# Decoder attention: the attended rows turned, divided and joined on VectorE in 32x32 blocks

## The chip, the cores and the metric

The kernel runs on one core of a Trainium2 chip. The metric is the device time of one execution in microseconds (us). The engines are TensorE (PE, with its weight loads as PEld), VectorE (DVE), ScalarE (ACT), GpSimd (POOL) and SyncE (SP), which issues the transfers. Each runs its own instructions in the order in which the program gives them, and they meet at semaphores.

## The reference

A decoder of four layers, then a cross attention and a mixture of experts, each with a residual and a norm. The change is in the decoder's attention alone:

```python
L, D, H, F = (4, 256, 16, 1024); HD = D // H
def mha(x, mask, Wi, bi, Wo, bo):
    B, T, _ = x.shape
    q, k, v = jnp.split(x @ Wi.T + bi, 3, axis=-1)
    # each: reshape(B, T, H, HD).transpose(0, 2, 1, 3)
    scores = jnp.einsum('bhqd,bhkd->bhqk', q, k) / math.sqrt(HD)
    attn = jax.nn.softmax(scores + mask[None], axis=-1)
    out = jnp.einsum('bhqk,bhkd->bhqd', attn, v)
    return out.transpose(0, 2, 1, 3).reshape(B, T, D) @ Wo.T + bo
for i in range(L):
    x = x + mha(layer_norm(x, ln1_w[i], ln1_b[i]), mask, ...)
    h = gelu(layer_norm(x, ln2_w[i], ln2_b[i]) @ ffn1_w[i].T + ffn1_b[i])
    x = x + (h @ ffn2_w[i].T + ffn2_b[i])
```

x is 16 x 256 tokens of 256 features, in float32.

## The kernel before

The 4096 tokens go in eight groups of 512 (`GT`), four layers long: 32 items n. The order of work is written out by hand for each engine in a function `body`, and one body works at four items: it prepares item n + 1 (`ahead`: first norm, queries and keys, maxima of the first two clusters), attends for item n (`front`), brings item n - 1 from its attended rows to the hidden layer (`back`), and shrinks the hidden layer of item n - 2 (`tail`). A steady body has all four. Three bodies in each layer also bring in the next layer's weights: `swap` 1 those of queries, keys and values, 2 those of the output projection, 3 those of the hidden layer; ACT and DVE make two float16 parts of each.

The 16 heads go in four clusters c of four heads (`C`), and the scores of a cluster in three stages s (`ST`). PE's `row_scores(n, c, s)` writes scores into the one bank pair `maxima_pair`; DVE's `maxima(n, c, s)` reduces them to the maximum of each row, and only then may PE write the next. PE's `key_scores(n, c, s)` writes the scores the other way round, maximum included, into the one pair `scores_pair`; ACT's `exps` makes the probabilities, and only then may PE write the next. POOL clears what lies ahead in time (`past_only`). PE's `attend(n, c)` multiplies with the values into the bank `O`: head u of the cluster has the partitions 32u to 32u + 31, of which 16 hold its attended features and the next one the sum of its probabilities, since `VS` has ones beside the values. So `O` is (head, feature) x 512 tokens. ACT's `out_rows(n, c)` copies it into `OTs[:, c, :]`.

In the next body the four copies are turned twice on PE. `turn_outputs` (line 735) makes four transposes of 128x128 into one bank for each 128 tokens t: tokens on the partitions. DVE's `outputs` (line 1160) takes the reciprocal of the sums and multiplies into `On`. `turn(..., "OT", k, ...)` (line 644) turns `On` back, half k of the 256 features at a time, into a bank; ACT's `outputs_high` and DVE's `outputs_low` add the values' bias and leave two float16 parts in `oT`, and PE's `attended` is the output projection.

All that PE writes for one reader, but scores and `O`, goes round a ring of three banks. `tiles_of` lists the uses in a body's order, and `free_tile` lets PE wait for the readers of the use three places before. After `attended` come DVE's addition into x, the second norm (`norm2_stats`, `norm2_root`, `norm2_scaled`), its turn on PE, the hidden layer (`hidden`, eight banks) with ACT's `gelu`, and the low parts by POOL (four) and DVE (four, `hidden_low`, line 1135, at the end of DVE's body). `norm1` for item n + 2 stands just ahead of these.

Of the kernel before, what the change touches and what calls it, by code (L numbers as in the profile page):

```python
# [17 lines left out]
P = 128  # L18
D = 256
# [331 lines left out]
def decoder(nc, sb, sem, psum, shared, dram):  # L351
# [36 lines left out]
    mx, mrow, PR, OTs, On, oT = (shared[k] for k in ("mx", "mrow", "PR", "OTs", "On", "oT"))  # L388
    rden = shared["rden"]
# [3 lines left out]
    def sig(name, per, unit=1):  # L393
        return Signal(sem("d_" + name), per, unit)
# [19 lines left out]
    OS_ps, rd_in, on_in = sig("OS_ps", TT), sig("rd_in", TT), sig("on_in", TT)  # L414
    OT_ps, oh, ol = sig("OT_ps", KD), sig("oh", KD), sig("ol", KD)
# [17 lines left out]
        "OS": [(on_in, 1)], "OT": [(oh, 1), (ol, 1)], "OP": [(xo, 1)], "T2": [(xf2, 1), (xh2, 1)],  # L433
# [3 lines left out]
    ROUND = {"T1": 1, "QK": 1, "MT0": 1, "MT1": 1, "V": 0, "MT2": 0, "MT3": 0, "OS": -1, "OT": -1, "OP": -1,  # L437
# [197 lines left out]
    def _(pe):  # L635
        for s in (T1_ps, V_ps, QK_ps, M_ps, MT_ps, S_ps, O_ps, OS_ps, OT_ps, OP_ps, T2_ps, H_ps, Y_ps):
            pe.sem_inc(s.sem, s.credit())
# [97 lines left out]
        def turn_outputs(kind, n, t):  # L735

            bank = free_tile(pe, kind, n, "OS", t)
            if t == 0:
                pe.wait_ge(o_in.sem, o_in.after(n - 1))
            for c in range(C):  # L740
                last = pe.transpose(bank[:, c * P:(c + 1) * P], OTs[:, c, t * P:(t + 1) * P], ident[:, :])
            last.then_inc(OS_ps.sem, 1)

# [27 lines left out]
        def body(kind, n, g, swap, l, ahead, front, back, tail):  # L771
# [9 lines left out]
            if back:  # L781
                turn_outputs(kind, n, 0)
                turn_outputs(kind, n, 1)
            if front:
                key_scores(n, 0, 1)
            if back:
                turn_outputs(kind, n, 2)
                turn_outputs(kind, n, 3)
            if front:
                row_scores(n, 2, 1)  # L790
                values(kind, n, 1)
            if back:
                pe.wait_ge(on_in.sem, on_in.after(n - 1))
                turn(kind, n, "OT", 0, OT_ps, On)
# [6 lines left out]
            if back:  # L801
                turn(kind, n, "OT", 1, OT_ps, On)
# [91 lines left out]
    def _(act):  # L894
# [58 lines left out]
        def outputs_high(kind, n, k):  # L953
            act.wait_ge(OT_ps.sem, OT_ps.after(n - 1, k + 1))
            if k == 0:
                act.wait_ge(OP_ps.sem, OP_ps.after(n - 2))
            act.activation(oT[0][:, k, :], tile(kind, "OT", k)[:, :], ACT.Identity, bias=value_col(n - 1, k))\  # L957
               .then_inc(oh.sem, 1)
# [163 lines left out]
    def _(dve):  # L1122
        for s in (w_lo, qb_ready, ln1_steps, z1, xl1, mx_in, rd_in, on_in, ol, xo, ln2_steps, z2, xl2, y_x, h_l[1],
                  *start.stats_in, start.rooted, start.zf, start.z1):
            dve.sem_inc(s.sem, s.credit())
# [34 lines left out]
        def outputs(kind, n, t):  # L1160
            dve.wait_ge(OS_ps.sem, OS_ps.after(n - 1, t + 1))
            bank = tile(kind, "OS", t)[:, :].rearrange("p (h d) -> p h d", h=H)
            if t == 0:
                dve.wait_ge(OT_ps.sem, OT_ps.after(n - 2))
            dve.reciprocal(rden[:, t, :], bank[:, :, HD]).then_inc(rd_in.sem, 1)
            dve.wait_ge(rd_in.sem, rd_in.after(n - 1, t + 1))
            dve.tensor_tensor(On[:, t, :].rearrange("p (h d) -> p h d", h=H), bank[:, :, 0:HD],
                              rden[:, t, :].unsqueeze(2).to_broadcast([P, H, HD]), ALU.mult)\
               .then_inc(on_in.sem, 1)

# [15 lines left out]
        def outputs_low(kind, n, k):  # L1186
            dve.wait_ge(oh.sem, oh.after(n - 1, k + 1))
            if k == 0:
                dve.wait_ge(OP_ps.sem, OP_ps.after(n - 2))
            dve.scalar_tensor_tensor(oT[1][:, k, :], tile(kind, "OT", k)[:, :], value_col(n - 1, k), oT[0][:, k, :],  # L1190
                                     ALU.add, ALU.subtract).then_inc(ol.sem, 1)
# [24 lines left out]
        def body(kind, n, g, swap, l, ahead, front, back, tail):  # L1216
# [14 lines left out]
            if back:  # L1231
                outputs(kind, n, 0)
                outputs(kind, n, 1)
                outputs(kind, n, 2)
                outputs(kind, n, 3)
# [29 lines left out]
            if back:  # L1265
                norm2_root(n, group(g, -1))
                norm2_scaled(n, group(g, -1))
            if swap == 2:
                weights(l, "o")
# [16 lines left out]
            if tail:  # L1286
                shrunk(kind, n, group(g, -2), 3)
            if swap == 3:
                weights(l, "f2")
            if ahead:  # L1290
                maxima(n + 1, 1, 0)
                maxima(n + 1, 1, 1)
                maxima(n + 1, 1, 2)
                if not (kind is STEADY and isinstance(n, int) and n + 2 >= L * NG):
                    if kind is PRE:
                        dve.wait_ge(s_x, 16)
                    norm1(n + 2, group(g, 2))
            if kind is LAST:
# [1634 lines left out]
def laid_out(inputs):  # L2933
# [7 lines left out]

    def columns(b):
        return b.reshape(-1, P).T
# [8 lines left out]
        stationary(f["attn_out_proj_w"][l].T),  # L2952
# [5 lines left out]
    value_cols = np.concatenate([*(columns(b[2 * D:]) for b in f["attn_in_proj_b"]), columns(f["xattn_bv"])], 1)  # L2958
# [35 lines left out]
```

## Time and profile before

| | |
|---|---|
| time, median of three runs | 3473.02 us (3469.25 to 3474.62) |
| the profiled execution: time, span | 3473.01 us, 3471.3 us |
| mean granted clock of TensorE | 0.970 |
| busy in the span: PE, DVE, ACT, POOL | 94%, 77%, 66%, 47% |
| ends of the last `out_rows`, first and last item | 89.8 us, 1768.4 us |
| between these, 23 of 31 bodies | 52.4 to 52.7 us each |
| three with `swap` 1 | 55.74, 57.73, 58.51 us |
| four with `swap` 3 | 63.35, 63.12, 63.62, 63.63 us |
| the last | 46.16 us |

The decoder takes the first half of the span. The lengths of its bodies are read from the starts of ACT's fourth `out_rows` in each. A busy PE is read with care: the ends of matmuls are modelled, so that a short wait can be hidden by the record of the matmul ahead of it, and the starts of the next instructions tell more. Idle time of an engine that nothing waits for costs nothing.

### The profile page before, as it was taken

What the parts mean: (1) busy time and instruction counts of PE and PEld (TensorE: products, weight loads), DVE (VectorE), ACT (ScalarE), POOL (GpSimd) and SP (SyncE); (2) the same over time, 40 slices, a digit from 0 to 9 for tenths busy, and PEclk for the clock granted to TensorE, in tenths of its full rate; (3) what the DMA queues carried; (4) which work ended last, traced back from release to release, by engine and by line L of the source; (5) the groups of instructions that cost most, each with busy time, mean ns of one, the idle gap of its engine ahead of it and who ended that gap; (6) DMA issues with size and microseconds to landing.
All of it is one profiled execution on the core that took longest, in us unless ns stands there. A gap on an engine that the chain in (4) does not pass through costs nothing. (4 is left out here: it accounts for less than half of the span.)

```text
span 3471.3 us, 76257 instructions
## 1 busy us (share of the span) xinstructions
PE 3252.6 (94%) x29568; PEld 2158.1 (62%) x29568; DVE 2675.1 (77%) x5237; ACT 2299.8 (66%) x3540; POOL 1648.4 (47%) x1612
## 2 busy tenths in 40 slices
PE   5899999999999999999986887899999999999998
PEld 2566665666656666566653554566666666666665
DVE  4777777777777777777677888898888888888877
ACT  3677776777777777777745665566666666666665
POOL 2354453544535445353444433564444444544475
PEclk8999999999999999999997999899999999999999
DMA  3110111101111011110011212100000000000001
GB/s 117 37 38 29 41 52 34 38 29 41 49 37 38 29 41 49 37 38 29 29 45 59 65 55 69 59 13 27 27 1 27 1 27 1 27 1 27 1 13 37
DMA packets 104485, 122.87 MB, mean 35 GB/s; under 512 B 20320, under 2 KB 92256, under 8 KB 101984
## 3 DMA queue, kind: packets, MB, share of 16 engines
q1 hardware_dynamic: 104128, 118.00, 10.4%
q8 instruction: 237, 3.88, 0.5%
q14 instruction: 120, 0.98, 0.1%
HBM read 49.35 MB, written 8.39 MB: 17 GB/s over the span
## 5 line engine op out<-in xcount | busy, mean ns | idle before, releaser
L2830 POOL TENSOR_TENSOR e_hT<-e_h,e_hT 128x512 f16<-128x512 f32 x512 | 613.5, 1200 | 605.7 <-ACT e_hT L2579 581.9
L1335 POOL TENSOR_SCALAR_AFFINE_SELECT PR<-PR 128x512 f32<-128x512 f32 (+1 forms) x384 | 307.4, 805 | 833.9 <-ACT PR L1002 832.1
L2573 ACT ACTIVATE e_h<-e_h,e_b 128x512 f32<-128x512 f32 x512 | 365.4, 714 | 416.3 <-DVE e_h L2659 416.3
L1214 DVE TENSOR_REDUCE mx<-maxima_pair 128x4 f16<-128x1024 f32 (+1 forms) x384 | 469.2, 1222 | 213.5 <-PE maxima_pair L694 213.4
L93 PE MATMUL bank<-xT,w_half 128*128 128x512 f16 x2400 | 568.5, 387 | 5.7 <-DVE xT L1157 4.2
L1002 ACT ACTIVATE PR<-scores_pair 128x1024 f32<-128x1024 f32 x384 | 391.6, 1020 | 102.4 <-PE scores_pair L706 101.9
L93 PEld LDWEIGHTS bank<-xT,w_half 128*128 128x128 f16 x2400 | 227.6, 99 | 272.6 <-issue 31.3
L2517 PE MATMUL bank<-VS,e_hT 128*128 128x256 f16 x3072 | 389.1, 273 | 6.2 <-DVE VS L2622 4.6
L2517 PE MATMUL bank<-e_w,e_hT 128*128 128x256 f16 x3072 | 388.7, 273 | 4.3 <-POOL e_hT L2830 4.1
L93 PE MATMUL bank<-w_half,hT 128*128 128x256 f16 x3072 | 364.3, 276 | 8.0 <-ACT oT L957 5.8
L2517 PEld LDWEIGHTS bank<-VS,e_hT 128*128 128x128 f16 x3072 | 300.2, 98 | 113.1 <-DVE VS L2622 5.1
L2517 PEld LDWEIGHTS bank<-e_w,e_hT 128*128 128x128 f16 x3072 | 300.7, 98 | 109.6 <-POOL e_hT L2830 6.3
L93 PEld LDWEIGHTS bank<-w_half,hT 128*128 128x128 f16 x3072 | 298.0, 99 | 63.4 <-issue 6.7
L2579 ACT ACTIVATE e_hT<-e_h 128x512 f16<-128x512 f32 x512 | 322.5, 630 | 16.2
L2669 DVE SCALAR_TENSOR_TENSOR x<-e_b,expert_weight,x 128x256 f32<-128x256 f32 x224 | 239.2, 1117 | 0.0
L1355 POOL TENSOR_TENSOR x<-x,spare 128x256 f32<-128x256 f32 x256 | 205.2, 837 | 18.9 <-DVE z L160 18.9
L1344 POOL TENSOR_TENSOR QK<-qk,QK 128x512 f16<-128x512 f32 x128 | 149.1, 1165 | 114.4 <-ACT qk L930 105.1
L995 ACT ACTIVATE spare<-bank,cols 128x512 f32<-128x512 f32 x256 | 172.7, 683 | 38.9 <-PE bank L93 38.4
L690 PE MATMUL maxima_pair<-KS,QS 63*128 63x256 f16 (+1 forms) x2048 | 152.3, 248 | 47.4 <-DVE mx L1214 41.7
L2659 DVE TENSOR_TENSOR e_h<-maxima_pair,e_common 128x512 f32<-128x512 f32 x192 | 131.1, 688 | 78.4 <-PE maxima_pair L2495 35.1
L2659 DVE TENSOR_TENSOR e_h<-scores_pair,e_common 128x512 f32<-128x512 f32 x192 | 131.9, 687 | 66.4 <-PE scores_pair L2495 50.3
L986 ACT ACTIVATE hT<-bank,cols 128x512 f16<-128x512 f32 x256 | 171.8, 686 | 8.0 <-PE bank L93 4.3
(215 smaller groups left out, 6352.2 us busy)
## 6 DMA issues: line engine op xcount, KB each, us to landing
QS<-QK SPq DMA_DIRECT2D x240, 128.0 KB, 2.1
KS<-QK SPq DMA_DIRECT2D x192, 128.0 KB, 2.1
PR<-in_expert_weights SPq DMA_DIRECT2D x16, 1024.0 KB, 5.1
stage<-in_weights SPq DMA_DIRECT2D x48, 256.0 KB, 3.4
xT<-in_x SPq DMA_DIRECT2D x8, 512.0 KB, 3.8
xT_f<-xT SPq DMA_DIRECT2D x8, 512.0 KB, 3.7
stage<-xT_f SPq DMA_DIRECT2D x4, 1024.0 KB, 5.2
out<-stage SPq DMA_DIRECT2D x8, 512.0 KB, 3.7
```

Source lines behind the costliest of these rows:

```text
L93: last = pe.matmul(out, stat(a, k), mov(b, k), start=(k == 0 and n == 0), stop=(k == tiles - 1 and n == 2))
L995: act.activation(h32[:, m % NH32, :], tile(kind, "H", m)[:, :], ACT.Gelu, bias=cols[:, COL["f1b"] + m:COL["f1b"] + m + 1], scale=1.0 / WS) ...
L1002: act.activation(PR[c % 2][:, s, :], SC[:, :], ACT.Exp).then_inc(p_in.sem, 1)
L1214: dve.tensor_reduce(out, src, AX.X, ALU.max, negate=True).then_inc(mx_in.sem, 1)
L1335: pool.affine_select(blocks, blocks, [[0, x], [1, P]], base=0, channel_multiplier=-1, compare_op=ALU.is_ge, fill=nothing).then_inc(past.se ...
L1355: last = pool.tensor_tensor(x[:, bass.ds(g * TT + t, 1), :], x[:, bass.ds(g * TT + t, 1), :], rows[:, row, :].unsqueeze(1), ALU.add)
L2517: last = pe.matmul(y_bank(tile), hT[r % 2][a][:, f, tile * P:(tile + 1) * P], w2[e % 2][b][:, i + f * NI, :], start=i == f == n == 0 and u ...
L2573: act.activation(h32[r % 2][:, j, :], h32[r % 2][:, j, :], ACT.Gelu, bias=b1[:, e, m:m + 1], scale=1.0 / WS)\
L2579: act.activation(hT[r % 2][0][:, f, t * GT:(t + 1) * GT], h32[r % 2][:, j, :], ACT.Copy).then_inc(h_h.sem, 1)
L2659: dve.tensor_tensor(out, bank_of(r, p), part, ALU.add).then_inc(added.sem, 1)
L2669: dve.scalar_tensor_tensor(x[:, n:n + 1, :], b2[e % 2][:, :, :], weight[:, at:at + 1], x[:, n:n + 1, :], ALU.mult, ALU.add).then_inc(bias_ ...
L2830: pool.tensor_tensor(hT[r % 2][1][:, f, part], h32[r % 2][:, j, :], hT[r % 2][0][:, f, part], ALU.subtract)\
```

## The change

The turns of the attended rows on PE are gone, and with them two uses of the ring of banks (`OS`, `OT`). ACT's copy in `OTs[:, c, :]` stays as it is. DVE's new `divide(n, c)` transposes each 32x32 block of it into `turned`: now a block has 32 tokens on its partitions and one head's 32 rows in its columns. The reciprocal of column 16 and a multiplication with the 16 features go into half of the 32 columns of each block in `divided`, which is a view of `On`; a cluster c takes the half c % 2. `join_outputs(n, k)` transposes two divided clusters in blocks once more, into `OTs[:, 2k, :]`: features on the partitions. ACT and DVE read that in place of a bank. The features come out in another order, so the output projection's weights and the values' bias are put in that order on the host.

The clusters are worked at as they come: `divide(n, 0)` after the second norm, `divide(n, 1)` and the first join ahead of the maxima of the next item's second cluster, `divide(n, 2)` after `norm1`, `divide(n, 3)` and the second join at the opening of the next body. ACT's `out_rows` waits until the rows that it overwrites have been read.

```diff
-        "OS": [(on_in, 1)], "OT": [(oh, 1), (ol, 1)], "OP": [(xo, 1)], "T2": [(xf2, 1), (xh2, 1)],
+        "OP": [(xo, 1)], "T2": [(xf2, 1), (xh2, 1)],
...
-        out = f(("V", 0)) + b(("OS", 0, 1, 2, 3)) + f(("V", 1)) + b(("OT", 0)) + a(("T1", 0)) + b(("OT", 1))
+        out = f(("V", 0, 1)) + a(("T1", 0))
...
         def out_rows(n, c):
             act.wait_ge(O_ps.sem, O_ps.after(n, c + 1))
-            if c == 0:
-                act.wait_ge(OS_ps.sem, OS_ps.after(n - 1))
+            if c % 2 == 0:
+                act.wait_ge(oh.sem, oh.after(n - 1, c // 2 + 1))
+                act.wait_ge(ol.sem, ol.after(n - 1, c // 2 + 1))
+            else:
+                act.wait_ge(turned_in.sem, turned_in.after(n - 1, c + 1))
             act.activation(OTs[:, c, :], O[:, :], ACT.Copy).then_inc(o_in.sem, 1)
...
+        def divide(n, c):
+            dve.wait_ge(o_in.sem, o_in.after(n, c + 1))
+            dve.wait_ge(on_in.sem, on_in.after(n, c))
+            dve.transpose(turned[:, :], OTs[:, c, :]).then_inc(turned_in.sem, 1)
+            blocks = turned[:, :].rearrange("p (b r) -> p b r", r=SQ)
+            dve.wait_ge(turned_in.sem, turned_in.after(n, c + 1))
+            dve.reciprocal(rden[:, c, :], blocks[:, :, HD]).then_inc(rd_in.sem, 1)
+            dve.wait_ge(rd_in.sem, rd_in.after(n, c + 1))
+            dve.wait_ge(joined.sem, joined.after(n - 1, c // 2 + 1))
+            to = divided[:, c // 2, :].rearrange("p (b r) -> p b r", r=SQ)[:, :, c % 2 * HD:(c % 2 + 1) * HD]
+            dve.tensor_tensor(to, blocks[:, :, 0:HD], rden[:, c, :].unsqueeze(2).to_broadcast([P, BL, HD]), ALU.mult)\
                .then_inc(on_in.sem, 1)
+        def join_outputs(n, k):
+            dve.wait_ge(on_in.sem, on_in.after(n, 2 * k + 2))
+            dve.transpose(OTs[:, 2 * k, :], divided[:, k, :]).then_inc(joined.sem, 1)
```

On PE at the opening of a steady body the turns stood between the values and the second `key_scores` and `row_scores`. Before, `scores_pair` is `key_scores`, `maxima_pair` is `row_scores`, and `OTs` is a turn:

```order
L93 MATMUL bank<-w_half,xT_1 128x256
L741 MATMUL bank<-ident,OTs 128x128 x8
L706 MATMUL scores_pair<-QS,KS 128x256 x4
L741 MATMUL bank<-ident,OTs 128x128 x8
L690 MATMUL maxima_pair<-KS,QS 128x256 x4
L694 MATMUL maxima_pair<-ident_b,mask_q 128x2x64 x4
```

and now:

```order
L93 MATMUL bank<-w_half,xT_0 128x256 x2
L93 MATMUL bank<-w_half,xT_1 128x256
L711 MATMUL scores_pair<-QS,KS 128x256 x4
L695 MATMUL maxima_pair<-KS,QS 128x256 x4
L699 MATMUL maxima_pair<-ident_b,mask_q 128x2x64 x4
```

The second `key_scores` and `row_scores` follow the values at once.

On DVE, across the end of a steady body and the opening of the next (`z` is the end of the first norm, `hT` is `hidden_low`, `mx` a maximum), before; the last two rows stand three times more ahead of the next maximum:

```order
L160 TENSOR_SCALAR z<-x,norm_mean_var,norm_root 128x256 x4
L1140 TENSOR_TENSOR hT<-spare,hT 128x512 x4
L1214 TENSOR_REDUCE mx<-maxima_pair 128x4
L1165 RECIPROCAL rden<-bank 128x16
L1167 TENSOR_TENSOR On<-bank,rden 128x256
```

and now:

```order
L160 TENSOR_SCALAR z<-x,norm_mean_var,norm_root 128x256 x4
L1150 STREAM_TRANSPOSE turned<-OTs 128x512
L1153 RECIPROCAL rden<-turned 128x16
L1157 TENSOR_TENSOR On<-turned,rden 128x16x16
L1126 TENSOR_TENSOR hT<-spare,hT 128x512 x4
L1208 TENSOR_REDUCE mx<-maxima_pair 128x4
L1150 STREAM_TRANSPOSE turned<-OTs 128x512
L1153 RECIPROCAL rden<-turned 128x16
L1157 TENSOR_TENSOR On<-turned,rden 128x16x16
L1163 STREAM_TRANSPOSE OTs<-On 128x512
L1208 TENSOR_REDUCE mx<-maxima_pair 128x4
```

One cluster is divided ahead of `hidden_low`, and another one divided and joined between the first two maxima.

On DVE after the second norm of a steady body (`x` is the addition of `shrunk`), before:

```order
L160 TENSOR_SCALAR z<-x,norm_mean_var,norm_root 128x256 x4
L1183 SCALAR_TENSOR_TENSOR x<-bank,x 128x256 x2
L1214 TENSOR_REDUCE mx<-maxima_pair 128x4
L1157 TENSOR_TENSOR xT_1<-xT_1,xT_0 128x512
L1214 TENSOR_REDUCE mx<-maxima_pair 128x4
```

and now:

```order
L160 TENSOR_SCALAR z<-x,norm_mean_var,norm_root 128x256 x4
L1150 STREAM_TRANSPOSE turned<-OTs 128x512
L1153 RECIPROCAL rden<-turned 128x16
L1157 TENSOR_TENSOR On<-turned,rden 128x16x16
L1177 SCALAR_TENSOR_TENSOR x<-bank,x 128x256 x2
L1208 TENSOR_REDUCE mx<-maxima_pair 128x4
```

A division stands ahead of the two additions, which free banks of the ring.

## Rows read from the trace of the kernel before

**Rows 1.** Busy time of bodies: length, PE, PEld, DVE, ACT, POOL, clock, DMA

```profile
691.47:743.92 52.45, 52.21 (x570) 34.39 (x566) 38.30 (x86) 39.56 (x59) 24.77 (x28) 1.00 0.10 32
415.19:470.93 55.74, 52.36 (x570) 34.43 (x566) 40.36 (x90) 41.22 (x62) 24.78 (x28) 1.00 0.19 63
849.39:907.12 57.73, 54.03 (x568) 35.30 (x566) 40.70 (x89) 41.23 (x62) 24.89 (x28) 0.97 0.19 61
523.46:586.58 63.12, 54.93 (x569) 34.97 (x566) 45.66 (x94) 43.76 (x67) 25.92 (x28) 0.95 0.14 46
```

**Rows 2.** Groups over the decoder: busy us, mean ns | idle before

```profile
L741 PE MATMUL bank<-ident,OTs 128*128 128x128 f32 x512 | 75.2, 281 | 11.8 <-DVE On L1167 7.5 <-ACT OTs L1008 0.8
L649 PE MATMUL bank<-ident,On 128*128 128x128 f32 x256 | 41.4, 287 | 0.8 <-DVE On L1167 0.8
L1167 DVE TENSOR_TENSOR On<-bank,rden 128x256 f32<-128x256 f32 x128 | 54.3, 424 | 4.4
L1165 DVE RECIPROCAL rden<-bank 128x16 f32<-128x16 f32 x128 | 31.6, 247 | 1.0 <-PE bank L741 1.0
L1157 DVE TENSOR_TENSOR xT<-xT 128x512 f16<-128x512 f32 x64 | 44.5, 696 | 59.0 <-ACT xT L913 59.0
```

**Rows 3.** Timeline of TensorE, a steady body's opening: start, length

```profile
691.47 0.39 PE L706 MATMUL scores_pair<-QS,KS 64*128 64x256 f16 x4
...
693.45 1.04 PE L741 MATMUL bank<-ident,OTs 128*128 128x128 f32 x8
694.61 0.39 PE L706 MATMUL scores_pair<-QS,KS 64*128 64x256 f16 x4
...
696.36 0.39 PE L690 MATMUL maxima_pair<-KS,QS 63*128 63x256 f16 x4
...
699.32 0.39 PE L690 MATMUL maxima_pair<-KS,QS 63*128 63x128 f16 x8
...
700.38 2.78 PE L93 MATMUL bank<-w_half,hT 128*128 128x256 f16 x24
```

**Rows 4.** Timeline of ScalarE, the same opening

```profile
692.24 1.28 ACT L1002 ACT_TABLE_LOAD   x1
693.53 1.02 ACT L1002 ACTIVATE PR<-scores_pair 128x1024 f32<-128x1024 f32 x1
```

**Rows 5.** Timeline of VectorE, the same opening

```profile
691.47 2.49 DVE L1140 TENSOR_TENSOR hT<-spare,hT 128x512 f16<-128x512 f32 x4
693.88 1.22 DVE L1214 TENSOR_REDUCE mx<-maxima_pair 128x4 f16<-128x1024 f32 x1
```

**Rows 6.** Timeline of all engines, the turn of the second norm

```profile
720.21 0.42 DVE L1183 SCALAR_TENSOR_TENSOR x<-bank,x 128x256 f32<-128x256 f32 x1
...
721.32 0.60 PE L649 MATMUL bank<-ident,z 128*128 128x128 f32 x4
```

**Rows 7.** Timeline of all engines, ahead of the next cluster's maxima

```profile
729.79 0.41 DVE L1183 SCALAR_TENSOR_TENSOR x<-bank,x 128x256 f32<-128x256 f32 x1
...
730.75 1.23 DVE L1214 TENSOR_REDUCE mx<-maxima_pair 128x4 f16<-128x1024 f32 x1 [0.55 <-PE maxima_pair L694]
...
733.34 0.39 PE L690 MATMUL maxima_pair<-KS,QS 63*128 63x256 f16 x4
```

**Rows 8.** Timeline of all engines, a collision of POOL and DVE

```profile
715.78 1.09 POOL L1335 TENSOR_SCALAR_AFFINE_SELECT PR<-PR 128x1024 f32<-128x1024 f32 x1 [1.35 <-ACT PR L1002]
...
715.88 1.00 DVE L150 SCALAR_TENSOR_TENSOR norm_root<-norm_slope,norm_root 128x4 f32<-128x4 f32 x1
```

**Rows 9.** Busy time around a fall of the clock, columns as in rows 1

```profile
421.55:425.00 3.45, 1.72 (x21) 1.33 (x19) 1.75 (x3) 2.90 (x6) 0.00 (x0) 1.00 0.00 0
858.45:861.87 3.42, 1.30 (x19) 1.06 (x20) 3.36 (x5) 2.25 (x5) 1.09 (x1) 1.00 0.00 0
861.87:865.29 3.42, 3.42 (x19) 2.44 (x17) 1.94 (x3) 1.30 (x2) 0.00 (x0) 0.50 0.00 0
```

**Rows 10.** Timeline of TensorE, opening of a body with a layer's first weights

```profile
860.57 0.40 PE L690 MATMUL maxima_pair<-KS,QS 63*128 63x128 f16 x8 [3.07 <-DVE mx L1214]
```

More of the change, by code:

```diff
@@ L387, in decoder @@
     qk32 = shared["qk32"]
-    mx, mrow, PR, OTs, On, oT = (shared[k] for k in ("mx", "mrow", "PR", "OTs", "On", "oT"))
-    rden = shared["rden"]
+    mx, mrow, PR, OTs, oT = (shared[k] for k in ("mx", "mrow", "PR", "OTs", "oT"))
+    SQ = 32
+    BL = GT // SQ
+    turned = sb("turned", [P, GT], F32)
+    rden = shared["rden"].rearrange("p c k -> p (c k)").rearrange("p (c k) -> p c k", c=C)
+    divided = shared["On"].rearrange("p t d -> p (t d)").rearrange("p (k n) -> p k n", k=KD)
+    assert C == 2 * KD and BL == H
     h32 = shared["spare"][:, 0:NH32 * GT].rearrange("p (m n) -> p m n", m=NH32)
@@ L635, in _ @@
     def _(pe):
-        for s in (T1_ps, V_ps, QK_ps, M_ps, MT_ps, S_ps, O_ps, OS_ps, OT_ps, OP_ps, T2_ps, H_ps, Y_ps):
+        for s in (T1_ps, V_ps, QK_ps, M_ps, MT_ps, S_ps, O_ps, OP_ps, T2_ps, H_ps, Y_ps):
             pe.sem_inc(s.sem, s.credit())
@@ L733, in attend @@
             last.then_inc(O_ps.sem, 1)
[L735 to L742, printed above, removed]
         def attended(kind, n, k):
@@ L800, in body @@
                 row_scores(n, 2, 2)
-            if back:
-                turn(kind, n, "OT", 1, OT_ps, On)
             if tail:
@@ L953, in outputs_high @@
         def outputs_high(kind, n, k):
-            act.wait_ge(OT_ps.sem, OT_ps.after(n - 1, k + 1))
+            act.wait_ge(joined.sem, joined.after(n - 1, k + 1))
             if k == 0:
                 act.wait_ge(OP_ps.sem, OP_ps.after(n - 2))
-            act.activation(oT[0][:, k, :], tile(kind, "OT", k)[:, :], ACT.Identity, bias=value_col(n - 1, k))\
+            act.activation(oT[0][:, k, :], OTs[:, 2 * k, :], ACT.Identity, bias=value_col(n - 1, k))\
                .then_inc(oh.sem, 1)
@@ L1122, in _ @@
     def _(dve):
-        for s in (w_lo, qb_ready, ln1_steps, z1, xl1, mx_in, rd_in, on_in, ol, xo, ln2_steps, z2, xl2, y_x, h_l[1],
+        for s in (w_lo, qb_ready, ln1_steps, z1, xl1, mx_in, turned_in, rd_in, on_in, joined, ol, xo, ln2_steps, z2, xl2, y_x, h_l[1],
                   *start.stats_in, start.rooted, start.zf, start.z1):
@@ L1231, in body @@
             if back:
[L1232 to L1235, printed above, removed]
+                divide(n - 1, 3)
+                join_outputs(n - 1, 1)
             if swap == 1:
@@ L1267, in body @@
                 norm2_scaled(n, group(g, -1))
+            if front:
+                divide(n, 0)
             if swap == 2:
@@ L1287, in body @@
                 shrunk(kind, n, group(g, -2), 3)
+            if front:
+                divide(n, 1)
+                join_outputs(n, 0)
             if swap == 3:
@@ L1297, in body @@
                     norm1(n + 2, group(g, 2))
+            if front:
+                divide(n, 2)
             if kind is LAST:
@@ L2940, in stationary @@
         return w.reshape(-1, P, w.shape[1]).transpose(1, 0, 2).reshape(P, -1)
+    turned = np.arange(D).reshape(KD, 2, C, HD).transpose(0, 2, 1, 3).reshape(D)
     def columns(b):
@@ L2957, in laid_out @@
     rows = np.stack([f["attn_out_proj_b"], f["attn_ffn2_b"]], 1)
-    value_cols = np.concatenate([*(columns(b[2 * D:]) for b in f["attn_in_proj_b"]), columns(f["xattn_bv"])], 1)
+    value_cols = np.concatenate([*(columns(b[2 * D:][turned]) for b in f["attn_in_proj_b"]), columns(f["xattn_bv"])], 1)
     wide = [(0, D - E_CTX), (0, 0)]
```

30 lines of the change are left out of this document (5 added, 25 removed).

## The prediction

> **What bounds the kernel now.** I read the busy times of single decoder bodies first, then the timelines of TensorE (PE), ScalarE (ACT) and VectorE (DVE) through one body, and at the end the clock. In a steady body PE shows 52.21 of 52.45 us busy at clock 1.00, DVE 38.30, ACT 39.56, POOL 24.77 [rows 1]. So PE sets the length of these bodies; 23 of the 31 listed in the table of the section on the profile have it. DVE's idle quarter is not spread evenly, though. I call S the start of a body on PE, 691.47 in [rows 3], and count from it. At S + 0.00 DVE is still at four `hidden_low` operations of the body before, which take 2.49 us; only then does it start the maximum of cluster 2, stage 0, at S + 2.41, for 1.22 us [rows 5]. PE reaches the next `row_scores`, which needs that maximum, at S + 4.89 (696.36). ACT, after a table load of 1.28 us, ends the first exponential at S + 3.08 [rows 4], and the second `key_scores` starts at S + 3.14 (694.61) [rows 3]. So at the opening ACT and DVE are late already, and the turns of the outputs on PE fill the time in which it would wait for them. Everywhere else I ask the same of each place that gets new work on DVE: how much later may DVE be there until PE notices?
>
> **What is removed.** Per body 16 transposes of the attended rows and 8 of the divided ones: 75.2 and 41.4 us in all [rows 2], 116.6 us or 3.64 us in each of the 32 bodies. On DVE four reciprocals of 0.247 us and four divisions of 0.424 us go from the opening [rows 2], and four of each come back elsewhere. ACT keeps its number of operations; the two biased copies of the attended features now read SBUF instead of a bank.
>
> **What is added.** Per body six block transposes of 128x512 on DVE. None stands in the trace. The nearest rows by shape are the DVE subtractions of 128x512, 0.696 us [rows 2]. Half of the columns take 0.424 us (128x256, [rows 2]); 1024 columns take 1.22 us [rows 5]. So T, the time of one, lies between 0.42 (two columns in the time of one) and 1.22 (two passes); I take 0.70, the row of the same shape. The Trainium skill, "Vector Engine (DVE) Microarchitecture Reference", section 3.8 on the reshape front-end, says that the transpose is pipelined to one element per cycle and lane; no run here shows it, and by it the upper end would fall away and the sum stay.
>
> A `divide` is then T, a reciprocal (0.25), a division (0.42), each waiting for the last: in [rows 5] an operation that waits for nothing starts 0.08 before the record of the one ahead ends (691.47 + 2.49 against 693.88), and I give 0.03 for a hand-over inside. This makes 0.70 + 0.03 + 0.25 + 0.04 + 0.42 - 0.08 = 1.36 us. `join_outputs` adds 0.73: 2.09 for both. Three places decide.
>
> *The opening.* `divide(n, 2)` now stands ahead of the four `hidden_low`: they end 1.36 later, the maximum starts at S + 3.77 and ends at 4.99, and PE's `row_scores` starts at S + 5.05. PE itself has done its first scores and values by S + 1.98 (693.45 [rows 3]), waits for ACT until 3.14, does 0.31 us of `key_scores`, and waits for DVE until 5.05: it loses 1.16 + 1.60 us. Behind that maximum DVE does `divide` of cluster 3 and the second join (2.09) where four reciprocals and divisions stood, so the next maximum starts at 3.77 + 1.14 + 2.09 = 7.00 and ends at 8.22: the third `row_scores` at S + 8.28, against 7.85 (699.32) before. It needs 0.54 us; the second turn of divided rows that followed it (0.52) is gone, and `shrunk` starts at S + 8.82, against 8.91 (700.38) before. So of 3.64 us removed, 0.09 us is left.
>
> *After the second norm.* `divide(n, 0)` stands ahead of the addition of `shrunk` 1 (720.21 to 720.63), which frees the bank for the turn of the second norm. That turn starts at 721.32 [rows 6], so the addition had 0.69 us to spare; 1.36 less 0.64 (with a hand-over of 0.05) makes 0.72 us of wait.
>
> *Ahead of the next cluster's maxima.* `divide(n, 1)` and the first join follow the addition that ends at 730.20; the maximum of cluster 1, stage 0, starts at 730.12 + 2.09 = 732.21, against 730.75, and with its 1.23 us is over at 733.44; PE wants it at 733.34 [rows 7]. That is 0.1 us, and I take 0.2, since the division there may meet POOL. In [rows 8] a DVE operation of two SBUF operands and 4 columns took 1.00 us: until POOL's operation ended. The division used to read a bank and now reads two SBUF operands. The Trainium skill, "SBUF — State Buffer", section "Who interferes with whom", has this as a lock between such an instruction and a GpSimd one that reads SBUF, and says that an instruction with one SBUF input takes no part in it; the row bears out the first half, and by the rule the six transposes are exempt.
>
> Sum of a steady body: -0.09 + 0.72 + 0.20 = +0.83 us; for 23 bodies +19.1. In the three bodies with the first weights of a layer (415.19, 849.39) the third `row_scores` already waits 3.07 us [rows 10] for maxima behind the weights on DVE, which wait for ACT and for the values; that stays, 0.16 later, and the turn's 0.52 is saved: -0.35 + 0.72 + 0.20, three times, +1.7. In the four with the hidden layer's weights (523.46) DVE waits for ACT's weights in the third place, which covers the join; I put +0.9 for each, +3.6.
>
> **The clock.** PE was at full clock (1.00) through the steady bodies. In 858.45 to 861.87 PE was busy 1.30 of 3.42 us, and the granted clock stood at 0.50, the lower level of 1.2 GHz, for the next 3.42 us; after 421.55 to 425.00, with 1.72 of 3.45 busy, it did not fall [rows 9]. The new opening has some 0.4 us busy in the 3.07 us from S + 1.98. It looks more like the first. Two bodies of the same work, one with such a fall and one without, last 57.73 and 55.74 us [rows 1]: a fall costs 1.99 us. Here some 0.6 of it falls into the wait for the third `row_scores`. Of the three bodies with that wait two show a fall; I take half of the steady bodies at 1.5 us: 23 x 0.75 = +17.
>
> All together 19.1 + 1.7 + 3.6 + 17 = +41.4 us. The profiled execution took 3473.01 us (span 3471.3), the median of the runs is 3473.02, so nothing is to be scaled: 3514.4.
>
> **Rivals.**
> 1. *The clock holds.* Same waits, no fall in the openings: 3473.0 + 24.4 = 3497.4. For it: each of the two waits is shorter than the 3.07 us of [rows 10], and work lies between them. Against: the sum of both in one stretch.
> 2. *The block transpose is slow.* At T = 1.22 the opening holds three of them in a chain (+1.56), the second place one (+0.52), the third two (+1.04): +3.12 per body beyond the 0.83, 23 x 3.95 = 91, falls in nearly all openings (+28) and some 16 in the other bodies: about 3608. For it: a 32-bit element may take two passes. Against: every DVE row follows its columns.
> 3. *The block transpose is quick, and the kernel gets faster.* At T = 0.42 the opening ends 0.84 earlier (-0.93), the second place costs 0.44, the third nothing: -0.49 per body, no long wait, 23 x -0.49 = -11: 3462. The point: without falls of the clock a body breaks even where 4 x (0.70 - T) = 0.63, T = 0.54. Against: no DVE row of 512 columns is that quick.
> 4. *The removed turns show in full*, DVE having room all along as its 73% busy suggests: 3473.0 - 116.6 = 3356. Against: the order of DVE's queue, worked out above. Partial forms lie between.
>
> **How the numbers follow.** Forecast with falls of the clock 0.43; clock holds 0.22; slow transpose 0.12; quick 0.13; full or large gain 0.04; the small terms cancel and nothing can be seen 0.06. A measurement of this kernel tells about 0.2% (7 us) from no change. Faster: quick and full, 0.17, less 0.01 of "quick" that ends within 0.2%: 0.16. Same: 0.06 and that 0.01, 0.07. Slower: 0.77. The range must hold 0.8: the forecast, the holding clock, no change (0.71), most of the quick case and the lower part of the slow one, so 3460 to 3600.
>
> **What would show it.** STREAM_TRANSPOSE of 128x512 at 0.70 us, 192 of them in the decoder. In a steady body the second `row_scores` 5.0 us and the third 8.3 us after the body's start, each released by DVE's maximum; the turn of the second norm released by DVE's addition, 0.7 us late; POOL's and ACT's lists unchanged; bodies of 53.3 us at full clock and about 55 where the clock falls behind the opening. DVE busy goes up by 32 x (6 x 0.70) = 134 us, PE's down by less than 117. Wrong would be: a transpose under 0.54 us, a steady body under 52.4, or PE without waits at the opening.

## The result: 84.7 us slower, twice the forecast loss

The changed kernel takes 3557.57 us (median of four runs, 3556.77 to 3560.1) against 3472.9 us: 1.0249 times the kernel before, 95% interval 1.0237 to 1.0261. The forecast was 3514.4. The direction held, the size did not: +84.7 us where the sum said +41.4.

The profiled execution (span 3556.0 us, of before 3471.3) has the whole difference in the decoder. The last `out_rows` of the decoder starts at 1850.6 us instead of 1768.4 (the table ahead of the prediction calls these starts ends), +82.2 us; what follows takes 1705.4 us instead of 1702.9. Busy time of the engines on the page of the changed kernel:

```profile
PE 3209.3 (90%) x28800; PEld 2097.2 (59%) x28800; DVE 2819.8 (79%) x5429; ACT 2304.8 (65%) x3540; POOL 1675.4 (47%) x1612
```

PE has 43 us less to do and DVE 145 us more, still with a fifth of the span free. The groups that are new, over the decoder (busy us, mean ns | idle before):

```profile
L1150 DVE STREAM_TRANSPOSE turned<-OTs 128x512 f32<-128x512 f32 x128 | 89.9, 702 | 0.0
L1163 DVE STREAM_TRANSPOSE OTs<-On 128x512 f32<-128x512 f32 x64 | 45.5, 711 | 2.2
L1157 DVE TENSOR_TENSOR On<-turned,rden 128x256 f32<-128x256 f32 x128 | 68.8, 538 | 4.9 <-DVE rden L1153 0.5
L1153 DVE RECIPROCAL rden<-turned 128x16 f32<-128x16 f32 x128 | 32.5, 254 | 4.4
```

The block transpose, the price that no row of before had, takes 0.70 us as taken. The division rose from 0.424 [rows 2] to 0.538 us in the mean, which comes back below.

Busy time of bodies, columns as in [rows 1]: a steady body in which the clock held, the next one, in which it fell, one with a layer's first weights (`swap` 1), one with the hidden layer's (`swap` 3):

```profile
723.45:777.35 53.90, 49.59 (x545) 31.75 (x542) 42.89 (x92) 39.74 (x59) 25.59 (x28) 1.00 0.09 31
777.35:832.68 55.33, 51.15 (x544) 32.53 (x541) 42.87 (x91) 39.73 (x59) 25.59 (x28) 0.97 0.09 30
429.46:490.82 61.36, 54.19 (x544) 34.15 (x541) 45.32 (x96) 41.28 (x62) 25.87 (x28) 0.89 0.18 57
546.68:613.07 66.39, 53.49 (x544) 32.91 (x540) 50.45 (x99) 43.81 (x67) 27.40 (x28) 0.92 0.13 43
```

Against 52.45, 55.74 and 63.12 [rows 1] every kind of body is longer, though each has 24 transposes less on PE. In the steady body PE is busy for 49.59 of 53.90 us; the other 4.31 us are five waits. The three of the opening, on TensorE, answer to [rows 3] (S is 723.45):

```profile
726.59 0.39 PE L711 MATMUL scores_pair<-QS,KS 64*128 64x256 f16 x4 [1.00 <-ACT PR L985]
728.50 0.39 PE L695 MATMUL maxima_pair<-KS,QS 63*128 63x256 f16 x4 [1.52 <-DVE mx L1208]
...
731.72 0.40 PE L695 MATMUL maxima_pair<-KS,QS 63*128 63x128 f16 x8 [0.53 <-DVE mx L1208]
731.96 0.38 PE L699 MATMUL maxima_pair<-ident_b,mask_q 64*128 64x256 bf16 x4
732.27 2.79 PE L93 MATMUL bank<-w_half,hT 128*128 128x256 f16 x24
```

The second `row_scores` comes at S + 5.05, the third at S + 8.27, `shrunk` at S + 8.82: the forecast said 5.05, 8.28 and 8.82. The other two waits, the turn of the second norm [rows 6] and the place ahead of the next cluster's maxima [rows 7], all engines:

```profile
754.05 0.63 PE L654 MATMUL bank<-ident,z 128*128 128x128 f32 x4 [0.66 <-DVE x L1177]
...
763.91 0.94 DVE L1157 TENSOR_TENSOR On<-turned,rden 128x256 f32<-128x256 f32 x1
763.94 0.63 POOL L1334 TENSOR_SCALAR_AFFINE_SELECT PR<-PR 128x512 f32<-128x512 f32 x1
...
766.77 0.39 PE L695 MATMUL maxima_pair<-KS,QS 63*128 63x256 f16 x4 [0.60 <-DVE mx L1208]
```

The division next to POOL's selection took 0.94 us, and PE waits 0.60 us for the maximum behind it. In the next body the opening has the same first two waits, and then the clock falls. Busy time before and after that moment, columns as above:

```profile
778.97:782.38 3.41, 0.91 (x9) 0.33 (x7) 3.41 (x6) 2.97 (x4) 1.56 (x2) 1.00 0.00 0
782.38:785.79 3.41, 3.39 (x21) 2.39 (x22) 3.08 (x5) 0.00 (x0) 0.28 (x1) 0.50 0.03 7
```

PE was busy for 0.91 of 3.41 us at clock 1.00; then it has its work back to back, at 0.50, the lower level of 1.2 GHz. This happens in 17 of the 23 steady bodies. Summed over the decoder from 150 us on, the clock stands at 0.50 for 136.5 us, before the change for 37.5 us.

### The profile page after: what moved, and what is told of

It reads as the page before. It is cut to its first block and busy times, and to the rows that moved or that the text cites. A ratio compares the mean times of both kernels' runs of the same rounds, so it can differ in the third digit from the quotient of the medians.

```text
span 3556.0 us, 75196 instructions
## 1 busy us (share of the span) xinstructions
PE 3209.3 (90%) x28800; PEld 2097.2 (59%) x28800; DVE 2819.8 (79%) x5429; ACT 2304.8 (65%) x3540; POOL 1675.4 (47%) x1612
## 5 line engine op out<-in xcount | busy, mean ns | idle before, releaser
L1334 POOL TENSOR_SCALAR_AFFINE_SELECT PR<-PR 128x512 f32<-128x512 f32 (+1 forms) x384 | 325.1, 850 | 881.6 <-ACT PR L985 877.3
L711 PE MATMUL scores_pair<-QS,KS 64*128 64x256 f16 (+1 forms) x2048 | 152.5, 248 | 37.6 <-ACT PR L985 37.0
```

The lines of the kernel that those rows point to most:

```text
L1334: pool.affine_select(blocks, blocks, [[0, x], [1, P]], base=0, channel_multiplier=-1, compare_op=ALU.is_ge, fill=nothing).then_inc(past.se ...
```

## The experiments

The theory after the result: nothing is lost because DVE has more to do, but because each piece stands ahead of something that PE needs soon (place); a part of the loss is the clock, which falls where the pieces hold PE up. The rival: DVE's 3.6 us more per body are paid wherever they stand (load). All times are medians over three rounds, and ratios are to the kernel before in the same job.

| kernel | us | ratio, 95% interval | steady body, clock up | steady bodies with a fall |
|---|---|---|---|---|
| before | 3470 to 3473 | 1 | 52.45 | 0 of 23 |
| changed | 3557.57 | 1.0249 (1.0237 to 1.0261) | 53.90 | 17 |
| `div0` | 3510.22 | 1.0116 (1.0101 to 1.0131) | 52.60 | 15 |
| `div1` | 3534.62 | 1.0184 (1.0169 to 1.0199) | 53.23 | 18 |
| `div2` | 3482.42 | 1.0033 (1.0023 to 1.0043) | 52.52 | 0 |
| `late1` | 3549.33 | 1.0226 (1.0211 to 1.0242) | 53.77 | 17 |
| `quiet` | 3539.34 | 1.0195 (1.0178 to 1.0212) | 53.49 | 18 |
| `busy` | 3527.81 | 1.0164 (1.0149 to 1.0179) | 53.90 | 0 |
| `busyo` | 3543.80 | 1.0206 (1.0189 to 1.0223) | 53.89 | 14 |
| `free` | 3432.87 | 0.9892 (0.9877 to 0.9907) | 50.89 | 0 |
| `all3` | 3451.59 | 0.9942 (0.9927 to 0.9957) | 51.59 | 0 |
| `all3late` | 3438.35 | 0.9906 (0.9889 to 0.9922) | 51.10 | 0 |
| `best` | 3421.52 | 0.9858 (0.9843 to 0.9873) | 50.52 | 0 |

### One piece at a time, behind a maximum

In `div2` only the division that stood ahead of `hidden_low` moves:

```diff
                 maxima(n + 1, 1, 1)
+            if front:
+                divide(n, 2)
+            if ahead:
                 maxima(n + 1, 1, 2)
...
-            if front:
-                divide(n, 2)
             if kind is LAST:
```

> divide(n, 2) stands between the maxima of stages 1 and 2 of the next item's cluster 1, where DVE waited 2.0 us for PE, not ahead of hidden_low; nothing else differs from the changed kernel. Theory 'place': the opening's chain on DVE is 1.36 us shorter, second row_scores at 3.7 and third at 6.9 us after the body's start (5.05 and 8.27 before this edit), steady body 52.5 us, and as the waits of the opening shrink to 1.2, 0.2 and 0.6 us the clock does not fall behind it: 23 x (54.98 - 52.5) = 57 us less, some 7 more in the bodies with weights, 3493 us. Rival 'load': DVE simply has too much to do, the wait turns up again at the next maxima, 3550 or more.

Measured 3482.42 us, 75 us less than the changed kernel. TensorE at the opening of a steady body, S = 698.01:

```profile
701.15 0.39 PE L711 MATMUL scores_pair<-QS,KS 64*128 64x256 f16 x4 [1.00 <-ACT PR L985]
701.69 0.39 PE L695 MATMUL maxima_pair<-KS,QS 63*128 63x256 f16 x4 [0.15 <-DVE mx L1208]
...
704.91 0.40 PE L695 MATMUL maxima_pair<-KS,QS 63*128 63x128 f16 x8 [0.53 <-DVE mx L1208]
```

The wait for DVE of 1.52 us is 0.15 us, and with it every fall of the clock is gone from the steady bodies. One division (1.36 us in the forecast), at the end of a body, was worth 1.38 us in each body and the falls besides. The kernel is 11 us faster than the 3493 expected, mainly because the seven bodies with weights got 18 us shorter where some 7 were written.

In `div0` and `div1` the pieces after the second norm and ahead of the next cluster's maxima move in the same way:

```diff
-            if front:
-                divide(n, 0)
...
                 maxima(n + 1, 0, 0)
+            if front:
+                divide(n, 0)
```

> divide(n, 0) stands behind the first maximum of the next item, not ahead of the two additions that free banks. Theory 'place': the wait of 0.75 us for the turn of the second norm is gone in all steady bodies, 53.15 us where the clock does not fall; falls behind the opening stay. 23 x 0.75 and some 5 in the others: 3535 us. Rival 'load': the 1.36 us delay the next low part or maximum and PE waits there, 3555 us.

```diff
-            if front:
-                divide(n, 1)
-                join_outputs(n, 0)
...
                 maxima(n + 1, 1, 0)
+            if front:
+                divide(n, 1)
+                join_outputs(n, 0)
+            if ahead:
                 maxima(n + 1, 1, 1)
```

> divide(n, 1) and the first join stand behind the maximum of stage 0 of the next item's cluster 1, not ahead of it. Theory 'place': the wait of 0.60 to 0.70 us at the following row_scores is gone, 53.2 us where the clock does not fall, 3538 us in all. Rival 'load': the maximum of stage 1 or 2 comes late in its place, 3555 us.

`div1` came out as expected: the body is 0.67 us shorter, what the third place cost, and the falls stay. The division there still takes 0.87 us in the median, but no step of PE waits for it now. `div0` did better than expected, 3510 where 3535 was written: the wait at the turn is gone, as it should be, but the wait in the third place also went from 0.60 to 0.16 us, though nothing was changed there. All engines around it in a body of `div0`:

```profile
694.72 0.50 DVE L1157 TENSOR_TENSOR On<-turned,rden 128x256 f32<-128x256 f32 x1
694.88 0.83 POOL L1334 TENSOR_SCALAR_AFFINE_SELECT PR<-PR 128x512 f32<-128x512 f32 x1
...
697.13 0.39 PE L695 MATMUL maxima_pair<-KS,QS 63*128 63x256 f16 x4 [0.16 <-DVE mx L1208]
```

DVE comes 0.16 us ahead of POOL, and it is POOL's selection that is stretched, from 0.63 to 0.83 us. So the place's price seems to hang on who comes first there; the next run asks whether POOL makes it. The 0.44 us, in 23 bodies, are 10 of the 25 us; the falls in the steady bodies cost 17.5 us in place of 24.1, and what else came was not followed up.

### POOL out of the division's way

```diff
-                past_only(n, 3, 0)
+                past_only(n, 3, 0, 16)
+                past_only(n, 3, 1, 16)
             if ahead:
                 query_key_low(n + 1, 3)
             if front:
-                past_only(n, 3, 1)
                 past_only(n, 3, 2)
```

> The changed kernel with VectorE's and TensorE's program as it is, and GpSimd made quiet where divide(n, 1) falls: the causal selection of the first two parts of chunk 3 covers 16 of the 128 columns (the rest of the selection is left out), and query_key_low of tile 3 stands behind these two. Theory (collision: the division of divide(n, 1), 0.94 us where it starts beside GpSimd's writes, is what made the third place cost 0.70 us, not 0.20): the division takes 0.42 to 0.52 us, the row_scores behind it waits 0.10 to 0.20 us in place of 0.59, and a steady body without a fall of the clock is 53.3 to 53.5 us in place of 53.9; the whole is 3530 to 3552 us if falls come as often. Rival (the place itself, that the piece has four instructions ahead of the maximum whatever GpSimd does): wait 0.5 to 0.6 us, body 53.8 to 53.9 us.

The wait and the body came out as the collision theory has it; the division, 0.54 us, is just over the 0.52 expected, since it still begins beside a selection. All engines:

```profile
871.68 0.54 DVE L1157 TENSOR_TENSOR On<-turned,rden 128x256 f32<-128x256 f32 x1
871.70 0.63 POOL L1334 TENSOR_SCALAR_AFFINE_SELECT PR<-PR 128x64 f32<-128x64 f32 x2
...
874.13 0.39 PE L695 MATMUL maxima_pair<-KS,QS 63*128 63x256 f16 x4 [0.20 <-DVE mx L1208]
```

The wait is 0.20 instead of 0.60 us and the body 53.49 instead of 53.90 us. The Trainium skill, "SBUF — State Buffer", section "Who interferes with whom", calls this an exclusive lock between a VectorE instruction with two SBUF inputs and a GpSimd one that reads SBUF, in which the order of issue decides who is held up. The row of `div0` agrees, where POOL's selection is the one held up. In the changed kernel DVE's record begins 0.03 us ahead of POOL's and DVE is held up, so at that distance the records don't tell who was first. The joins, block transposes with one input, stay between 0.695 and 0.715 us, as the rule has it.

### The opening's own piece

In `late1` `divide(n - 1, 3)` and the second join go behind the second maximum of the opening:

```diff
-            if back:
-                divide(n - 1, 3)
-                join_outputs(n - 1, 1)
...
                 maxima(n, 2, 1)
+            if back:
+                divide(n - 1, 3)
+                join_outputs(n - 1, 1)
```

> The changed kernel with divide(n - 1, 3) and join_outputs(n - 1, 1) behind maxima(n, 2, 1) in the opening, all else as it is: the opening's piece alone. Theory (place): the second row_scores of chunk 2 still comes at 5.05 us after the body's first key_scores, since divide(n, 2) at the end of the body before makes it late; the third comes at 6.9 to 7.1 us in place of 8.27, but the output projection then waits for VectorE's outputs_low and starts at some 12.6 us, 0.3 to 0.5 us sooner than in the changed kernel. A steady body without a fall 53.4 to 53.7 us; falls in fewer of the bodies; 3515 to 3550 us. Rival (the opening's piece is the one that costs most, as it stands ahead of the maxima on which TensorE's first scores rest): second row_scores at 3.9 us or sooner, body 52.5 to 52.8 us, 3480 to 3505 us.

TensorE in a body with S = 782.24:

```profile
787.29 0.39 PE L695 MATMUL maxima_pair<-KS,QS 63*128 63x256 f16 x4 [1.52 <-DVE mx L1208]
...
794.80 0.93 PE L93 MATMUL bank<-w_half,oT 128*128 128x256 f16 x7 [0.41 <-issue]
```

The second `row_scores` is where it was, at S + 5.05, so the rival falls. The third comes at S + 7.58, where 6.9 to 7.1 was expected. The output projection starts at S + 12.56, as expected, but that is only 0.13 us sooner than in the changed kernel (S + 12.70), not 0.3 to 0.5: a miss in my reading of where it stood. Its wait takes the place of the one removed. The body is 53.77 us, just over the 53.7 expected, and falls came as often as before, in 17 bodies; that expectation was wrong too. With the division ahead of `hidden_low` still there, the waits of 1.00 and 1.52 us stay, and the falls with them.

### What the clock takes

`busy` leaves all waits as they are and gives PE matmuls that nobody reads, in the two waits of the opening:

```diff
                 values(kind, n, 0)
+                idle_matmuls(kind, n, 4)
                 key_scores(n, 0, 1)
+                idle_matmuls(kind, n, 6)
                 row_scores(n, 2, 1)
```

> The changed kernel with added work on PE: four matmuls of 128x512 ahead of the second key_scores and six ahead of the second row_scores, into a bank that the next values overwrite; all waits stay. Theory 'clock': the waits of the opening cost a second time, by falls of the clock in 17 of 23 steady bodies at some 1.3 us each; with PE busy there the clock stays at 1.00, all steady bodies last 53.9 us, 25 us less, and 5 to 10 less in the bodies with weights: 3525 us. Rival: the longer bodies have another cause (POOL, ACT), then ten more matmuls change nothing or cost up to 23 x 0.5 us: 3557 to 3570 us.

TensorE in the opening, S = 714.50:

```profile
716.48 1.03 PE L669 MATMUL bank<-xT,w_half 128*128 128x512 f16 x4
717.64 0.39 PE L716 MATMUL scores_pair<-QS,KS 64*128 64x256 f16 x4
717.97 1.47 PE L669 MATMUL bank<-xT,w_half 128*128 128x512 f16 x6
719.56 0.39 PE L700 MATMUL maxima_pair<-KS,QS 63*128 63x256 f16 x4
```

The second `row_scores` is at S + 5.06 again, the body is 53.91 us, and no steady body has a fall. PE does more and the kernel is 30 us faster than the changed one. By kind of body: the 23 steady ones take 22.6 us less in all, the three with `swap` 1 take 59.0 in place of 61.4 us, 7.0 less in all, the four with `swap` 3 the same.

Those four had lost 3.5 us each, and this does not explain it. TensorE at their output projection, of the changed kernel, and of the kernel before at the same work:

```profile
564.13 2.72 PE L93 MATMUL bank<-w_half,oT 128*128 128x256 f16 x12 [3.86 <-DVE oT L1184]
```

```profile
540.05 1.47 PE L93 MATMUL bank<-w_half,oT 128*128 128x256 f16 x12 [1.59 <-DVE oT L1190]
```

Before, PE waited 1.93 us ahead of `shrunk` and 1.59 us here, and had its clock; in two of the other three bodies the clock fell at `shrunk`, and the time that this cost was gone in the wait here. Now both are one wait of 3.86 us, and the projection runs at half speed. The first of the four had such a wait, 3.87 us, and such a fall before the change too. In `busyo` 14 matmuls that nobody reads fill it:

```diff
                     part_ready("o", l)
+                    bank = free_tile(pe, kind, n, "OP", 0)
+                    for _ in range(14):
+                        pe.matmul(bank[:, :], views["qkv"][0][:, 0, 0:P], views["qkv"][0][:, 0, 0:GT], start=True, stop=True)
                 attended(kind, n, 0)
```

> The changed kernel, with 14 matmuls of 128x512 more, whose result nobody reads, ahead of the output projection in the four bodies that load the hidden layer's weights: they fill most of its wait of 3.86 us (VectorE's outputs_low stands behind four pieces of the weights). Theory (the clock: those bodies lost 14.0 us in all, 5.8 of it the four steady terms, and the other 8.2 because the long wait, which turns of the outputs broke up before, now ends at half clock): the projection takes 1.4 to 1.6 us in place of 2.72, these bodies 64.6 to 65.6 us in place of 66.4 and 68.3, other bodies as in the changed kernel; 3545 to 3553 us. Rival (the 8.2 us are VectorE's, late by its new work): projection at half clock or not, these bodies stay at 66.2 us or more, 3555 to 3560 us.

```profile
557.91 3.19 PE L798 MATMUL bank<-w_half 128*128 128x512 f16 x14
561.66 1.47 PE L93 MATMUL bank<-w_half,oT 128*128 128x256 f16 x12 [0.57 <-issue]
```

The projection takes 1.47 us again. The four bodies took 65.90, 64.08, 63.83 and 65.33 us, 8.6 us less in all. The middle two are under the range expected; the first, over it, and the last have other falls in their openings. The whole is 1 us under its range.

### DVE's work left out, and all pieces moved

`free` has PE's program of the changed kernel and leaves out what DVE does for it:

```diff
-            if back:
-                divide(n - 1, 3)
-                join_outputs(n - 1, 1)
...
-            if front:
-                divide(n, 0)
...
-                act.wait_ge(joined.sem, joined.after(n - 1, k + 1))
+                act.wait_ge(o_in.sem, o_in.after(n - 1, 2 * k + 1))
```

> Left out: the whole of divide and join_outputs, so the attended rows are neither turned nor divided (outputs_high and outputs_low read OTs as ScalarE copied it). TensorE has the changed kernel's work, VectorE 3.6 us a body less. It measures what the removed transposes of TensorE are worth when what replaces them costs VectorE nothing. Theory (place): the opening is then bound by ScalarE (table load and exponentials before the second key_scores), so only 1.0 to 1.6 us of the 3.64 us of transposes show in a steady body: 50.8 to 51.4 us, and 3420 to 3450 us, within 20 us of the kernels whose pieces are all moved. Rival (load): 48.8 to 49.5 us a steady body, some 3360 us, so that VectorE's share is what keeps the others from it.

`all3` moves the three pieces that stand ahead of maxima, `all3late` the opening's as well, and `best` puts `outputs_low` of half 1 ahead of the first norm's `low`:

```diff
                 maxima(n + 1, 1, 0)
+            if front:
+                divide(n, 1)
+            if ahead:
                 maxima(n + 1, 1, 1)
+            if front:
+                join_outputs(n, 0)
+                divide(n, 2)
+            if ahead:
                 maxima(n + 1, 1, 2)
...
+            if back:
+                outputs_low(kind, n, 1)
             if ahead:
                 low(0, n + 1, 0, xh1, xf1, xl1)
-            if back:
-                outputs_low(kind, n, 1)
```

> All three pieces that stand ahead of a chunk of maxima of the next cluster move behind one: divide(n, 0) behind the first maximum of chunk 0, divide(n, 1) behind the first of chunk 1, join_outputs(n, 0) and divide(n, 2) behind the second of chunk 1; divide(n - 1, 3) stays in the opening. VectorE does the same instructions as in the changed kernel. Theory (place: each piece costs only what it makes the queue behind it late): the steady body without a fall of the clock, 53.9 us in the changed kernel, loses the four parts that the single moves showed, to 50.9 to 51.5 us, no falls in the 23 steady bodies, and the whole is 3435 to 3460 us, faster than the kernel before. Rival (load: the 3.6 us a body that VectorE has more to do are paid wherever they stand): a steady body of 52.5 us or more and 3475 us or more.

> As the kernel with the three pieces moved, and besides divide(n - 1, 3) and join_outputs(n - 1, 1) behind maxima(n, 2, 1) in the opening instead of ahead of it. Theory (place): the third row_scores of chunk 2 comes some 0.1 us sooner and shrunk 0.2 to 0.3 us sooner than with the three pieces alone, but ScalarE's outputs_high and VectorE's outputs_low then end the wait of the output projection, so 50.9 to 51.5 us a steady body, within 0.3 us of the kernel with three pieces, and 3430 to 3465 us. Rival (load): 52.5 us or more, 3475 us or more.

> As the kernel with the three pieces and the opening's piece moved, and besides outputs_low of half 1 ahead of low(0, n + 1, 0) on VectorE. Theory (place): the output projection then starts some 0.6 us sooner, a steady body of 50.2 to 51.2 us, 3410 to 3455 us, 0 to 25 us faster than without the swap. Rival (load): no change from it, 52.5 us or more.

Busy time of a steady body of `free`, `all3`, `all3late` and `best`, columns as above:

```profile
678.97:729.86 50.89, 49.32 (x546) 31.74 (x542) 36.07 (x78) 39.65 (x59) 24.82 (x28) 1.00 0.10 33
```

```profile
686.46:738.05 51.59, 49.31 (x544) 31.75 (x540) 43.35 (x91) 39.61 (x59) 25.26 (x28) 1.00 0.10 32
```

```profile
682.97:734.07 51.10, 49.32 (x545) 31.73 (x542) 43.02 (x91) 39.66 (x59) 25.31 (x28) 1.00 0.10 33
```

```profile
677.41:727.93 50.52, 49.16 (x545) 31.80 (x542) 43.07 (x91) 39.66 (x59) 25.30 (x28) 1.00 0.10 33
```

The load theory falls. DVE is as busy in `best` (43.07 us) as in the changed kernel (42.89 us), and the body is 3.38 us shorter; against `free` DVE has 7.0 us more and the body is 0.37 us shorter, since only `best` has the two `outputs_low` in the better order. `all3` stopped at 51.59, just over its expected 50.9 to 51.5: there the third `row_scores` waits 0.94 us, more than I had taken, and so `all3late`, which removes that wait, gives 0.49 us a body where 0.3 were expected at most. The swap in `best` gives another 0.58. TensorE in the opening of `best`, S = 677.41:

```profile
680.55 0.39 PE L711 MATMUL scores_pair<-QS,KS 64*128 64x256 f16 x4 [1.00 <-ACT PR L985]
681.30 0.39 PE L695 MATMUL maxima_pair<-KS,QS 63*128 63x256 f16 x4 [0.36 <-DVE mx L1208]
...
688.24 1.47 PE L93 MATMUL bank<-w_half,oT 128*128 128x256 f16 x12
```

What is left is 1.00 us for ACT's exponential and 0.36 us for a maximum. Of the 3.64 us of turns that PE no longer does, 1.93 us show (52.45 to 50.52), and the swap of `outputs_low`, 0.58 of them, was not tried in the kernel before. `best` is 1.4% faster than the kernel before and 3.8% faster than the changed one.

## Why the prediction was right and wrong

Forecast and profiled execution, in us (the body's parts are read at the starts of PE's instructions: how much later, counted from S, each comes than in the kernel before):

| term | forecast | measured |
|---|---|---|
| opening, up to `shrunk` and behind it | -0.09 | -0.07 |
| turn of the second norm | +0.72 | +0.85 |
| ahead of the next cluster's maxima | +0.20 | +0.67 |
| steady body, clock up | +0.83 | +1.45 |
| 23 of them | +19.1 | +33.4 |
| falls of the clock in them | +17 | +24.1 |
| three bodies with `swap` 1 | +1.7 | +12.2 |
| four with `swap` 3 | +3.6 | +14.0 |
| start, last body, all behind the decoder | 0 | +1.0 |
| sum | +41.4 | +84.7 |

**Right.** The block transpose at the price of the subtraction of its shape (0.70); the opening, where 3.64 us of PE's work went and the next steps come at the same time; who is waited for in each place; and that the clock would fall behind the opening. The Trainium skill, "Vector Engine (DVE) Microarchitecture Reference", section 3.8, has the transpose at one element per cycle and lane; the 0.70 us agree, the same as the 0.696 us of a subtraction of that shape.

**The third place was mis-sized**, 0.67 for 0.20. The step named the cause, that the division may meet POOL, and then put 0.1 us on it. It cost 0.4 us in each body, shown by `quiet` (53.90 to 53.49) and by chance in `div0`. The row of a collision was at hand [rows 8]; what I did not do was to look what POOL has at the new time of the division, though its timeline stood in the trace. The turn's 0.13 us more is small, and not followed up.

**The falls were mis-sized in number, not in price.** Forecast half of the bodies at 1.5 us, measured 17 of 23 at 24.1 / 17 = 1.42 us. `busy` and `div2`, each without a fall, show that it is the clock and that the wait of 1.52 us behind the one of 1.00 us brings it. Why six bodies with the same two waits have none is open.

**The bodies with weights were the step that failed.** I walked their waits for DVE and left the clock out; the sum of both kinds was 5.3 us, and 26.2 came. With `swap` 1, of 12.2 us the steady body's waits are 3 x 1.45 = 4.4, the clock 7.0 (`busy`), and 0.8 is left. In the first of them the clock stands at 0.50 for four times as long as a fall in a steady body, with two more long waits, 2.03 and 2.88 us, inside that time:

```profile
434.22:447.87 13.65, 9.97 (x64) 6.77 (x65) 8.93 (x13) 5.62 (x9) 1.92 (x2) 0.50 0.05 18
```

With `swap` 3, 14.0 us, I read the starts of PE's instructions as in the table, in the body from 546.68. The terms that I had put there come: the turn costs 0.85 us and the third place 0.24, where the weights cover the rest. What I had left out is twice as much: the output projection starts 0.85 us late, and its stretch at half clock adds 1.51; what follows takes back 0.18, so +3.27 in all. Of the 0.85 us, 0.44 are the weights' four pieces on DVE, before and now:

```profile
535.38 3.25 DVE L1131 SCALAR_TENSOR_TENSOR w_half<-stage,w_half 128x512 f16<-128x512 f32 x4
558.82 3.69 DVE L1117 SCALAR_TENSOR_TENSOR w_half<-stage,w_half 128x512 f16<-128x512 f32 x4
```

The last of the four now runs beside a selection of POOL, 1.12 us in place of 0.68. `free` has the same 3.69 us, so their new time does it and not DVE's new work. `busyo` takes 8.6 us from the four bodies. About 6.3 of these come by the end of the projection; the other 2.2 come behind the third place, mostly because the last fall of three bodies is 3.4 us long and not 6.8, its length before the change too. So about 6.3 of the 14.0 us are the clock at the projection, and 7.7 the rest, mostly waits for DVE (in the last of the four a fall in the opening too). That DVE's weights set the time there I had right; I said that this covers the join, and did not see that the turns on PE had cut a long wait into two. `free`, without DVE's new work, has the same wait of 3.87 us and the same projection at half clock, so it is the missing work of PE.

Together the clock took some 24.1 + 7.0 + 6.3 = 37 us of the 84.7, waits for DVE, with that rest, 33.4 + 4.4 + 7.7 = 46, and 2 are not assigned: 2.5 us come from behind the decoder, where kernels with the same code lie between 1697.4 and 1709.0 us, the rest from the smaller terms. A shorthand for the first: the Trainium skill, "TensorE: Matmul & The Clock Gate", section "Terms", puts the price of a throttled stretch at its time by the share of pulses left out. The 136.5 - 37.5 = 99 us more at half clock would by that cost 49.5 us. The runs show less, 37, because part of the slow work falls where PE would have waited: in the body from 777.35 the third `row_scores` has no wait left.

**The rivals.** That the clock holds gave 3497.4; `busy` is that case, 3527.8, for the mis-sized third place and the bodies with weights. That the gain shows in full did not come even where DVE does none of the new work (`free`, 3432.9 against 3356): ACT's exponential and the chain through `oT` end the opening's waits then. The transpose took 0.70 us, so neither the slow nor the quick one came.

## To carry to other kernels

An engine at 77% has room, but a queue has none ahead of an instruction for which the busiest engine waits: the same instructions cost 85 us or gave 32 (`all3late`), only by whether each stood ahead of a maximum or behind one, and gave 49 with `outputs_low` moved as well (`best`). When work is taken off the busiest engine, ask what its absence uncovers, also for the clock: the turns were useful as cover, and where PE then idles, its next work may run at half speed, as in 17 of the 23 steady bodies. For each instruction that comes to read two SBUF operands, look up what POOL does at its new time, and not only how long it takes alone.

## What I had not expected

- PE can do more and the kernel be faster: ten matmuls of 128x512 per body, read by nobody, took 30 us off (`busy`), 14 more in each of four bodies 14 us (`busyo`, 8.6 of them in those four).
- The turns on PE, 16 of attended and 8 of divided rows in fp32, kept the clock at 1.00 through the opening of all 23 steady bodies of the kernel before; without them, and with nothing in their place, it fell in 17.
- An edit can shift another place against POOL: `div0` changed nothing ahead of the next cluster's maxima, and 0.44 us went there, because DVE came 0.16 us ahead of POOL's selection instead of beside it.
